# Layer 0's adjacency masks: ScalarE converts two of a tile's four chunks instead of one, VectorE the other two

## The chip, the cores and the metric

The kernel runs on one core of one Trainium2 chip. The metric is the device time of one launch in microseconds (us); several runs of each kernel are taken, and one more execution is profiled. The core's engines are TensorE (PE; its weight loads are PEld), VectorE (DVE), ScalarE (ACT), GpSimd (POOL, idle here) and SyncE (SP), which issues every DMA. Each engine runs its own instructions strictly in the order of the program and waits on semaphores.

## The reference, cut to what matters

Two graph-attention layers over 8192 nodes with 128 features, with a residual after each. The adjacency `adj` is an 8192 x 8192 int32 matrix with about 8 ones in a row, 0.1% of its entries. Layer 0, the one changed here:

```python
h = maximum(layernorm(x), 0)
e = (h @ Ws) @ (h @ Wt).T
alpha = softmax(where(adj > 0, e, -9e15), axis=-1)
x = x + alpha @ (h @ Wc)
```

Layer 1 has the same form with scores `leaky_relu(s1[:, None] + s2[None, :])` and an elu at the end.

## The kernel before, in words

**Tiles and blocks.** A tile is 128 query rows; there are 64. For each tile the matrix `adjB` (a copy of `adj` in which a tile's block of 128 x 8192 lies transposed, key on the partitions) is read in 4 chunks of 16 blocks of 128 keys, 1 MB each. A tile has so few neighbours that layer 0 does not score all 8192 keys: for each block of 128 keys it picks those that are a neighbour of any row of the tile, at most 32, and gathers their keys, values and mask columns with one-hot matrices on TensorE. 64 blocks x 32 slots are 16 groups of 128 slots, on which scores, exponentials and the weighted sum are made.

**A tile's way through the engines** (functions by their names; all in the loop `tile_sweep`, line 332, whose step i handles tile i at its first stages and older tiles at the later ones):

- SP, `load_chunk` (413): loads chunk c of tile i + 1 into `adj_st[:, c]`. Each chunk has a single buffer, so SP first waits until the chunk of the tile before has been converted. `tile_io` (442) issues the four loads in order, then the stores of the one-hot matrix (`store_pick`), of the gathered mask (`store_mask`), of the finished rows, and the next load of rows.
- Conversion of a chunk from int32 to a one-byte mask `mask_8`: by VectorE in line 1327 (chunks 0, 1, 2; values +0.5 and -0.5) and by ScalarE in line 1019 (chunk 3; `Sign` gives +1 and -1). Two sets of constants undo the different scales: `bare` (1207, 1208) and `off_i[q // 3]` (713).
- VectorE, `indicate` (1330): waits for all four chunks, takes a maximum over the rows of each key (line 1334) and compares it with `bare` (1336). TensorE, `prefix` (700, matmul at 704): running count. VectorE, `place` (1338, line 1343): slot numbers `posx`. In the next step VectorE's `make_pick` (1345, line 1352) makes the one-hot matrix `pick`.
- TensorE gathers keys (`pick_keys`, 668), values (`pick_values`, 680) and mask (`pick_mask`, 695) in four, four and two parts, each into one PSUM bank that ScalarE copies out (`take_keys`, 990; `take_values`, 996; `take_mask`, 1003) before the next part may start. `pick_mask` 0 of step i also waits until `place` of tile i - 1 is done.
- TensorE, `scores` (706, lines 712, 713 and 718) for four groups of slots. VectorE takes two maxima (`part_maximum`, 1361), spreads them (`spread_maximum`, 1367), TensorE transposes (`turn_maximum`, 727), VectorE reduces (`maximum`, 1374, 1377). ScalarE makes the exponentials in two halves (`exps`, 1010); `scores` 2 and 3 of the next tile wait for the second half. TensorE, `weigh` (729, lines 736 and 739): 32 float32 matmuls of the sum. VectorE, `denominator` (1384) and `finish` (1391, 1394).

**The order around the change** is written out by hand in each engine's `tile_step`. With a = i - 2, c = i - 3, d = i - 4:

- PE (743): prefix(i-1), scores(c, 3), pick_values(c, 2), pick_mask(a, 0), pick_keys(a, 1), pick_values(c, 3), pick_mask(a, 1), turn_maximum(c), pick_keys(a, 2), pick_values(a, 0), weigh(d, 0 to 3), pick_keys(a, 3), scores(a, 0), pick_values(a, 1), scores(a, 1), pick_keys(i-1, 0), scores(a, 2).
- ACT (1022): take_values(c, 2), take_mask(a, 0), take_keys(a, 1), take_values(c, 3), take_mask(a, 1), take_keys(a, 2), convert(i), exps(c, 0), take_values(a, 0), take_keys(a, 3), exps(c, 1), take_values(a, 1), take_keys(i-1, 0).
- DVE (1397): spread_maximum(c), convert(i, 0), maximum(c), convert(i, 1), make_pick(i-1), convert(i, 2), denominator(d), indicate(i), finish(d), part_maximum(a, 0), place(i), part_maximum(a, 1).

The first six and the last six steps are unrolled; the rest is a hardware loop of two steps. Layer 1 runs after it, on the masks and one-hot matrices that layer 0 stored; the change does not touch it.

Of the kernel before, what the change touches and what calls it, by code (L numbers as in the profile page):

```python
# [13 lines left out]
ACT = mybir.ActivationFunctionType  # L14
# [28 lines left out]
NO_EDGES = struct.unpack("<f", bytes([0xB0] * 4))[0]  # L43
NO_EDGES_ACT = struct.unpack("<f", bytes([0xB8] * 4))[0]


def gnn_kernel(nc, x, adj, adjB, Ws, Wt, Wc, W1, a1, out, x_mid, sel, sel_pick):
    N = x.shape[0]
    TILES = N // P
# [5 lines left out]
    NB = TILES  # L55
    SB = NB // QB
    QCH = NB // 4
    assert CW == 2 * GW and TILES == 64 and D == P

    with ExitStack() as ctx:  # L60
# [11 lines left out]
        def part(start, words, dt=F32):  # L72
            view = arena[:, start:start + words]
            return view if dt == F32 else view.bitcast(dt)
# [4 lines left out]
        adj_st = part(ADJ, 8192, I32).rearrange("p (c b n) -> p c b n", c=4, n=P)  # L79
# [6 lines left out]
        mask_8 = part(MASK, 4096, F8).rearrange("p (r b n) -> p r b n", r=2, n=P)  # L86
# [8 lines left out]
        m_sel8 = part(MS, 1024, F8).rearrange("p (r s n) -> p r s n", r=2, n=P)  # L95
# [8 lines left out]
        off_i = [part(at, P // 2, BF16) for at in (TOP + 2752, END + 200)]  # L104
        bare = part(END + 264, NB)
# [141 lines left out]
        adj_in = [sem(f"adj_in{c}") for c in range(4)]  # L247
        conv_done = sem("conv_done")
        conv_act = sem("conv_act")
# [12 lines left out]
        mg_done = sem("mg_done")  # L262
# [61 lines left out]
        def wait(eng, s, value):  # L324
            if not (isinstance(value, int) and value <= 0):
                eng.wait_ge(s, value)
# [15 lines left out]
        def there(i, d):  # L342

            return within(i, d, TILES + d)
# [51 lines left out]
        def _(sp):  # L396
# [15 lines left out]

            def load_chunk(t, c):

                if c < 3:
                    wait(sp, conv_done, t * 3 + (c - 2))
                else:
                    wait(sp, conv_act, t)
                rows = adjB[bass.ds(t, 1), :, c * QCH:(c + 1) * QCH, :].rearrange("o p b n -> p (o b) n")
                sp.dma_start(adj_st[:, c, :, :], rows).then_inc(adj_in[c], 16)  # L420

# [20 lines left out]
            def tile_io(i, b):  # L442
                if within(i, 0, TILES - 1):
                    for c in range(4):
                        load_chunk(i + 1, c)
                if there(i, 1):
                    store_pick(i - 1, 1 - b)
                if there(i, 2):
                    store_mask(i - 2, b)
                if there(i, 4):  # L450
                    store_y(i - 4, b)
                if within(i, 4, TILES + 2):
                    load_x(i - 2, b)
                if isinstance(i, int) and i == TILES:
                    sp.wait_ge(conv_done, TILES * 3)
                    sp.wait_ge(conv_act, TILES)
                    sp.wait_ge(y_out[0], 16 * (3 * TILES // 8))
                    sp.wait_ge(y_out[1], 16 * (3 * TILES // 8))
                    load_rows(x_mid, 1, range(3))
# [129 lines left out]
        def _(pe):  # L589
# [116 lines left out]
            def scores(t, b, q):  # L706

                pe.wait_ge(k_evac, t * 4 + (q + 1))
                pe.wait_ge(m_evac, t * 2 + (q // 2 + 1))
                wait(pe, p_done, t * 2 + (q // 2 - 1))  # L710
                dst = s_ps[q]
                nc.tensor.matmul(dst, ones_b[:, :], negc, start=True, stop=False, skip_group_check=True)  # L712
                nc.tensor.matmul(dst, off_i[q // 3], m_sel8[:, b, 4 * q:4 * q + 4, :].rearrange("p s n -> p (s n)"),  # L713
                                 start=False, stop=False, skip_group_check=True)
                for k in range(4):
                    at = (4 * q + k) * P
                    for n, rows in enumerate((cq_hi, cq_lo)):
                        last = nc.tensor.matmul(dst[:, k * P:(k + 1) * P], k_sel[:, at:at + P],  # L718
                                                rows[:, bass.ts(t, P)], start=False, stop=(n == 1),
                                                skip_group_check=True)  # L720
                last.then_inc(sc_done, 1)
# [187 lines left out]
        def _(act):  # L909
# [77 lines left out]
            def take_keys(t, g):  # L987

                act.wait_ge(kg_done, t * 4 + (g + 1))
                nc.scalar.activation(k_sel[:, g * GW:(g + 1) * GW], kg_ps, ACT.Copy).then_inc(k_evac, 1)  # L990
# [20 lines left out]
                                     ps[:, 2 * h:2 * h + 2, :].rearrange("p b n -> p (b n)"), ACT.Exp,  # L1011
                                     bias=neg_max[:, 0:1], scale=1.0 / SCORE).then_inc(p_done, 1)

            def convert(t, b):

                act.wait_ge(adj_in[3], t * 16 + 16)
                wait(act, mg_done, t * 2 - 2)
                act.sem_inc(conv_settled, 1)
                nc.scalar.activation(mask_8[:, b, 3 * QCH:4 * QCH, :], adj_st[:, 3, :, :], ACT.Sign, bias=-0.5, saturate=False  # L1019
                                     ).then_inc(conv_act, 1)  # L1020

            def tile_step(i, b):
                a, c, cb = i - 2, i - 3, 1 - b
                if there(i, 3):
                    take_values(c, cb, 2)
                if there(i, 2):
                    take_mask(a, b, 0)
                    take_keys(a, 1)
                if there(i, 3):
                    take_values(c, cb, 3)  # L1030
                if there(i, 2):
                    take_mask(a, b, 1)
                    take_keys(a, 2)
                if there(i, 0):
                    convert(i, b)
                if there(i, 3):
                    exps(c, 0)
                if there(i, 2):
                    take_values(a, b, 0)
                    take_keys(a, 3)  # L1040
                if there(i, 3):
                    exps(c, 1)
                if there(i, 2):
                    take_values(a, b, 1)
                if there(i, 1):
                    take_keys(i - 1, 0)
# [138 lines left out]
        def _(dve):  # L1185
# [13 lines left out]
            def constants():  # L1199

                dve.wait_ge(const_pool, 4)
                dve.wait_ge(ident_ready, 1)
                nc.vector.tensor_copy(tri[:, :], tri_f[:, :])
                nc.vector.tensor_copy(slots[:, :], slot_i[:, :])
                for n in range(2):
                    nc.vector.tensor_scalar(off_i[n], ident[:, :], OFF * (4, 2)[n], None, ALU.mult)
                nc.vector.memset(bare[:, 0:3 * QCH], NO_EDGES)
                nc.vector.memset(bare[:, 3 * QCH:NB], NO_EDGES_ACT)
                nc.vector.memset(pos_top, 0.0)
                nc.vector.memset(negc, -2.0 * OFF / P).then_inc(const_dve, 1)  # L1210

# [110 lines left out]
            def convert(t, b, c):  # L1322

                dve.wait_ge(adj_in[c], t * 16 + 16)
                wait(dve, mg_done, t * 2 + (c // 2 - 3))
                settle()
                nc.vector.tensor_scalar(mask_8[:, b, c * QCH:(c + 1) * QCH, :], adj_st[:, c, :, :], 0.0, 0.5,  # L1327
                                        ALU.is_gt, ALU.subtract, saturate=False).then_inc(conv_done, 1)

            def indicate(t, b):  # L1330

                dve.wait_ge(conv_done, t * 3 + 3)
                dve.wait_ge(conv_act, t + 1)
                nc.vector.reduce_max(ind_raw[:, :], mask_w[:, b, :, :], AX_X).then_inc(ind_max, 1)  # L1334
                dve.wait_ge(ind_max, t + 1)
                nc.vector.tensor_tensor(ind[:, :], ind_raw[:, :], bare, ALU.is_gt).then_inc(ind_ready, 1)
# [60 lines left out]
            def tile_step(i, b):  # L1397
                e, a, c, d = i - 1, i - 2, i - 3, i - 4
                if there(i, 3):
                    spread_maximum(c)  # L1400
                if there(i, 0):
                    convert(i, b, 0)
                if there(i, 3):
                    maximum(c)
                if there(i, 0):
                    convert(i, b, 1)
                if there(i, 1):
                    make_pick(e, 1 - b)
                if there(i, 0):
                    convert(i, b, 2)  # L1410
                if there(i, 4):
                    denominator(d)
                if there(i, 0):
                    indicate(i, b)
                if there(i, 4):
                    finish(d, b)
                if there(i, 2):
                    part_maximum(a, 0)
                if there(i, 0):
                    place(i)  # L1420
                if there(i, 2):
                    part_maximum(a, 1)
# [351 lines left out]
```

## Time and profile before

| | |
|---|---|
| runs | 1467.81, 1470.81, 1476.16 us; median 1470.81 |
| profiled execution | 1470.75 us; its span from first to last instruction 1469.0 us |
| busy in the span | PE 1283.0 us (87%), DVE 1265.2 (86%), ACT 1039.5 (71%), POOL 1.5 |
| mean granted TensorE clock | 0.966 of full speed |
| layer 0's sweep | about 90 to 975 us of the span |
| layer 1 | about 1060 to 1469 us |
| DMA | 363.20 MB over the span |

A busy share is an average over stages with different limits, and an engine that is busy may still not be what the others wait for. The period of a repeating instruction and the waits by releaser say more. In the rows below a line of a timeline reads: start, length, engine, line of the kernel, operation, output and input, shape, count, and in brackets the idle time before it with what ended it. Ends of matmuls are modelled; differences between starts are firm. An instruction can start up to some 0.1 us before the end of the one before it on the same engine. "issue" is a wait for which the profile shows no releaser.

### The profile page before, as it was taken

The numbers are of one execution on the slowest core, as the hardware profiler recorded it, in microseconds if no ns is written. First come the engines' busy times: TensorE is split into PE (matmuls) and PEld (weight loads), VectorE is DVE, ScalarE is ACT, GpSimd is POOL, SyncE is SP. The second block draws the span as 40 slices with busy tenths as digits, with TensorE's granted clock in tenths as the row PEclk, the third lists the DMA queues.
The fourth block names the chain that finished last, engine by engine and source line by source line (L and its number), as shares of the span: only waits on it lengthen the run. The fifth ranks groups of instructions, "written<-read, shape, count | busy, mean of one in ns | idle before, by whom it ended". The sixth has DMA issues, their size and how long they took to land.

```text
span 1469.0 us, 75909 instructions
## 1 busy us (share of the span) xinstructions
PE 1283.0 (87%) x31819; PEld 1132.6 (77%) x31947; DVE 1265.2 (86%) x2313; ACT 1039.5 (71%) x2064; POOL 1.5 (0%) x11
## 2 busy tenths in 40 slices
PE   2827899999999999999999998967699999999996
PEld 1625778878888888888888887755499999999896
DVE  5877689999999999999999998634699999999996
ACT  2835567667677667676767676539599989998885
POOL 0000000000000000000000000000000000000000
PEclk9967899999999999999999999988899999999998
DMA  7049889999999999999999999440132444244432
GB/s 238 1 195 333 281 309 359 372 370 368 380 373 381 372 370 387 362 382 369 375 373 372 374 382 363 145 115 1 45 108 85 120 115 114 87 118 118 117 89 70
DMA packets 114312, 363.20 MB, mean 247 GB/s; under 512 B 11504, under 2 KB 44528, under 8 KB 81392
## 3 DMA queue, kind: packets, MB, share of 16 engines
q1 hardware_dynamic: 114160, 361.02, 68.9%
q8 instruction: 115, 1.88, 0.6%
q14 instruction: 37, 0.30, 0.1%
HBM read 319.03 MB, written 41.94 MB: 246 GB/s over the span
## 4 chain that ended last, share of the span: by engine, by line
PE 46%; DMA 19%; DVE 15%; issue 11%; ACT 7%; SPq 1%; DVEq 1%; ACTq 0%
DMA arena<-in_adjB 17%; PE ps L819 16%; PE ps L806 9%; PE ps L718 4%; DVE arena L1352 4%; DVE arena L1327 4%; PE ps L739 3%; PE ps L713 3%; PE ps L680 3%; DVE mx L1361 2%; ACT arena L1010 2%; ACT arena L915 2%; PE ps L668 2%; PE ps L712 1%; SPq L420 1%
## 5 line engine op out<-in xcount | busy, mean ns | idle before, releaser
L739 PE MATMUL ps<-arena 128*128 128x129 f32 x2048 | 253.1, 283 | 6.0 <-issue 6.0
L739 PEld LDWEIGHTS ps<-arena 128*128 128x128 f32 x2048 | 244.5, 198 | 6.2 <-issue 6.2
L819 PE MATMUL ps<-arena 128*128 128x129 f32 x2048 | 243.0, 277 | 1.1 <-issue 1.1
L996 ACT ACTIVATE arena<-ps 128x512 f32<-128x512 f32 x256 | 153.1, 598 | 125.3 <-PE ps L680 125.2
L1327 DVE TENSOR_SCALAR arena<-arena 128x2048 fp8e4<-128x2048 int32 x192 | 234.8, 1224 | 6.6 <-PE ps L695 3.1
L819 PEld LDWEIGHTS ps<-arena 128*128 128x128 f32 x2048 | 234.6, 192 | 1.4 <-issue 1.4
L1500 DVE TENSOR_SCALAR arena<-arena 128x128 f32<-128x128 f32 x768 | 202.5, 340 | 23.0 <-issue 14.0
L1019 ACT ACTIVATE arena<-arena 128x2048 fp8e4<-128x2048 int32 x64 | 122.3, 1911 | 97.8 <-DMA arena<-in_adjB 97.8
L990 ACT ACTIVATE arena<-ps 128x512 f16<-128x512 f32 x256 | 153.9, 601 | 50.4 <-PE ps L668 50.2
L718 PEld LDWEIGHTS ps<-arena 128*128 128x128 f16 x2048 | 137.5, 99 | 62.8 <-issue 3.6
L1361 DVE TENSOR_REDUCE mx<-ps 128x1 f32<-128x1024 f32 x128 | 155.8, 1217 | 34.0 <-PE ps L718 33.3
L680 PE MATMUL ps<-arena 128*32 128x128 f16 x8192 | 164.8, 222 | 13.4 <-issue 5.7
L1060 ACT ACTIVATE arena<-ps 128x396 f32<-128x396 f32 (+1 forms) x384 | 148.2, 463 | 25.8 <-PE ps L806 25.6
L806 PE MATMUL ps<-arena 128*32 128x132 f16 x8192 | 152.0, 224 | 14.8 <-ACT arena L1060 6.3
L1010 ACT ACTIVATE arena<-ps,neg_max 128x1024 f32<-128x1024 f32 x128 | 142.0, 1110 | 25.2 <-PE ps L739 25.1
L718 PE MATMUL ps<-arena 128*128 (+1 forms) x2048 | 157.9, 220 | 0.0
L806 PEld LDWEIGHTS ps<-arena 128*32 128x32 fp8e4 x8192 | 129.4, 97 | 33.9 <-issue 17.9
L1334 DVE TENSOR_REDUCE arena<-arena 128x64 f32<-128x2048 f32 x64 | 146.3, 2286 | 6.0 <-ACT arena L1019 3.5
L1509 DVE SCALAR_TENSOR_TENSOR arena<-arena 128x1024 f32<-128x1024 fp8e4 x128 | 151.0, 1217 | 0.5 <-ACT arena L1077 0.3
L668 PE MATMUL ps<-arena 128*128 128x32 fp8e4 x4096 | 143.3, 177 | 7.0 <-DVE arena L1352 6.6
L680 PEld LDWEIGHTS ps<-arena 128*32 128x32 fp8e4 x8192 | 121.1, 97 | 34.5 <-issue 17.9
L1352 DVE TENSOR_TENSOR arena<-arena 128x2048 fp8e4<-128x2048 f16 x64 | 146.2, 2284 | 0.1
(166 smaller groups left out, 1399.1 us busy)
## 6 DMA issues: line engine op xcount, KB each, us to landing
arena<-in_adjB SPq DMA_DIRECT2D x256, 1024.0 KB, 7.4
sel_pick<-arena SPq DMA_DIRECT2D x64, 256.0 KB, 9.4
sel<-arena SPq DMA_DIRECT2D x64, 256.0 KB, 9.5
arena<-sel_pick SPq DMA_DIRECT2D x64, 256.0 KB, 3.7
arena<-sel SPq DMA_DIRECT2D x64, 256.0 KB, 2.8
x_t<-in_x SPq DMA_DIRECT2D x64, 64.0 KB, 8.1
x_mid<-y_t SPq DMA_DIRECT2D x64, 64.0 KB, 8.4
arena<-x_mid SPq DMA_DIRECT2D x8, 512.0 KB, 5.0
```

Of the source, the lines that this page charges most:

```text
L668: last = nc.tensor.matmul(kg_ps[:, k * SLOT:(k + 1) * SLOT], kp[:, g * SB + k, :], pick[:, b, g * SB + k, :], start=True, stop=True)
L680: last = nc.tensor.matmul(vg_ps[j * SLOT:(j + 1) * SLOT, s * D:(s + 1) * D], pick[:, b, k, :], c_vals[:, k, l * D:(l + 1) * D], start=(l = ...
L718: last = nc.tensor.matmul(dst[:, k * P:(k + 1) * P], k_sel[:, at:at + P], rows[:, bass.ts(t, P)], start=False, stop=(n == 1), skip_group_c ...
L739: last = nc.tensor.matmul(pv_ps, p_T[:, s * P:(s + 1) * P], v_sel[:, b, s, :], start=False, stop=(s == SB - 1), skip_group_check=True)
L806: last = nc.tensor.matmul(xg_ps[g % 3][j * SLOT:(j + 1) * SLOT, at:at + XW], pick[:, b, s * QB + j, :], wv[:, s * QB + j, l, :], start=(l ...
L819: last = nc.tensor.matmul(xv_ps[b], w_msk[:, b, s, :], x1_sel[:, b, s, 0:VW], start=False, stop=(s == SB - 1), skip_group_check=True)
L990: nc.scalar.activation(k_sel[:, g * GW:(g + 1) * GW], kg_ps, ACT.Copy).then_inc(k_evac, 1)
L1010: nc.scalar.activation(p_T[:, h * 1024:(h + 1) * 1024], ps[:, 2 * h:2 * h + 2, :].rearrange("p b n -> p (b n)"), ACT.Exp, bias=neg_max[:, ...
L1327: nc.vector.tensor_scalar(mask_8[:, b, c * QCH:(c + 1) * QCH, :], adj_st[:, c, :, :], 0.0, 0.5, ALU.is_gt, ALU.subtract, saturate=False).t ...
L1352: nc.vector.tensor_tensor(pick[:, b, :, :], posx.unsqueeze(2).to_broadcast(wide), slots[:, :].unsqueeze(1).to_broadcast(wide), ALU.is_equa ...
L1361: nc.vector.reduce_max(mx[:, h:h + 1], ps[:, 2 * h:2 * h + 2, :].rearrange("p b n -> p (b n)"), AX_X).then_inc(part_max, 1)
L1500: last = nc.vector.tensor_scalar(w_raw[b][:, k, :], own, x1_sel[:, b, k, D + 2:D + 3], x1_sel[:, b, k, D + 1:D + 2], ALU.mult, ALU.max)
```

## The change: another split and another order of the conversions

ScalarE converts chunks 2 and 3. Chunk 2 stands where chunk 3 stood (before `exps(c, 0)`), chunk 3 after `take_keys(a, 3)` and before `exps(c, 1)`. VectorE loses `convert(i, 2)`, between `make_pick` and `denominator`. The counts on `conv_done` and `conv_act` become two a tile each, and the constants follow the new split.

```diff
 def load_chunk(t, c):
-    if c < 3:
-        wait(sp, conv_done, t * 3 + (c - 2))
-    else:
-        wait(sp, conv_act, t)
+    wait(sp, conv_act if c >= 2 else conv_done, t * 2 + (c % 2 - 1))
...
-nc.tensor.matmul(dst, off_i[q // 3], m_sel8[:, b, 4 * q:4 * q + 4, :]...
+nc.tensor.matmul(dst, off_i[q // 2], m_sel8[:, b, 4 * q:4 * q + 4, :]...
...
-def convert(t, b):
-    act.wait_ge(adj_in[3], t * 16 + 16)
+def convert(t, b, c):
+    act.wait_ge(adj_in[c], t * 16 + 16)
     wait(act, mg_done, t * 2 - 2)
...
 # ACT tile_step
     if there(i, 0):
-        convert(i, b)
+        convert(i, b, 2)
     if there(i, 3):
         exps(c, 0)
     if there(i, 2):
         take_values(a, b, 0)
         take_keys(a, 3)
+    if there(i, 0):
+        convert(i, b, 3)
     if there(i, 3):
         exps(c, 1)
...
-nc.vector.memset(bare[:, 0:3 * QCH], NO_EDGES)
-nc.vector.memset(bare[:, 3 * QCH:NB], NO_EDGES_ACT)
+nc.vector.memset(bare[:, 0:2 * QCH], NO_EDGES)
+nc.vector.memset(bare[:, 2 * QCH:NB], NO_EDGES_ACT)
...
 def indicate(t, b):
-    dve.wait_ge(conv_done, t * 3 + 3)
-    dve.wait_ge(conv_act, t + 1)
+    dve.wait_ge(conv_done, t * 2 + 2)
+    dve.wait_ge(conv_act, t * 2 + 2)
...
 # DVE tile_step
     if there(i, 1):
         make_pick(e, 1 - b)
-    if there(i, 0):
-        convert(i, b, 2)
     if there(i, 4):
         denominator(d)
     if there(i, 0):
         indicate(i, b)
```

## Rows read from the trace of the kernel before

**Rows 1.** Stage: length, PE, PEld, DVE, ACT, POOL busy us, clock, DMA share, GB/s

```profile
98.00:250.00 152.00, 118.13 (x3021) 101.65 (x3043) 117.98 (x147) 86.52 (x121) 0.00 (x0) 0.84 0.91 326
250.00:900.00 650.00, 609.31 (x16491) 537.60 (x16580) 611.74 (x803) 453.74 (x652) 0.00 (x0) 1.00 1.00 374
```

**Rows 2.** Line 1334: count, ns min/median/max, first and last start, in 98:250 and 250:900

```profile
L1334 DVE TENSOR_REDUCE arena<-arena x10: 2285/2286/2287, 106.8 to 242.1; 128x64 f32<-128x2048 f32 x10
...
L1334 DVE TENSOR_REDUCE arena<-arena x50: 2285/2286/2289, 254.9 to 890.8; 128x64 f32<-128x2048 f32 x50
```

**Rows 3.** Who waited for whom in 250:900: us in total, times, longest

```profile
ACT arena L1019 <- DMA arena<-in_adjB: 71.3, 50, 2.6
PE ps L713 <- ACT arena L1010: 32.1, 37, 1.8
...
DVE arena L1334 <- ACT arena L1019: 0.5, 2, 0.3
```

**Rows 4.** The chain that ended last, around 515 us: start, us, what

```profile
515.21 9.73 DMA arena<-in_adjB
```

**Rows 5.** DMA traffic in 250:900

```profile
DMA packets 57817, 242.99 MB, mean 374 GB/s; under 512 B 6424, under 2 KB 19244, under 8 KB 32198
```

**Rows 6.** VectorE in order of time: start, us, line, shape

```profile
513.31 1.22 DVE L1327 TENSOR_SCALAR arena<-arena 128x2048 fp8e4<-128x2048 int32 x1
...
514.65 2.29 DVE L1334 TENSOR_REDUCE arena<-arena 128x64 f32<-128x2048 f32 x1
...
518.94 0.21 DVE L1343 TENSOR_TENSOR arena<-ps,arena 128x64 f16<-128x64 f32 x1
...
520.69 0.29 DVE L1367 SCALAR_TENSOR_TENSOR arena<-mx 128x128 f32<-128x128 f32 x1
```

**Rows 7.** ScalarE in the same stretch; in brackets idle before, and releaser

```profile
514.92 0.60 ACT L990 ACTIVATE arena<-ps 128x512 f16<-128x512 f32 x1
515.40 1.12 ACT L1010 ACTIVATE arena<-ps,neg_max 128x1024 f32<-128x1024 f32 x1
...
517.63 0.60 ACT L990 ACTIVATE arena<-ps 128x512 f16<-128x512 f32 x1 [0.62 <-PE ps L668]
...
525.13 1.91 ACT L1019 ACTIVATE arena<-arena 128x2048 fp8e4<-128x2048 int32 x1 [1.97 <-DMA arena<-in_adjB]
526.95 1.10 ACT L1010 ACTIVATE arena<-ps,neg_max 128x1024 f32<-128x1024 f32 x1
```

**Rows 8.** TensorE in the same stretch

```profile
513.83 0.56 PE L668 MATMUL ps<-arena 128*128 128x32 fp8e4 x16
...
517.04 0.56 PE L668 MATMUL ps<-arena 128*128 128x32 fp8e4 x16
517.66 0.38 PE L713 MATMUL ps<-arena 128*128 128x512 fp8e4 x1
...
519.78 0.43 PE L695 MATMUL ps<-arena 128*32 128x64 f16 x32
...
521.66 0.33 PE L727 MATMUL ps<-ident,arena 128*128 128x128 f32 x1
...
526.58 0.56 PE L668 MATMUL ps<-arena 128*128 128x32 fp8e4 x16
528.32 0.38 PE L713 MATMUL ps<-arena 128*128 128x512 fp8e4 x1 [1.19 <-ACT arena L1010]
```

**Rows 9.** A tile in which VectorE waited for ScalarE's conversion

```profile
603.46 1.91 ACT L1019 ACTIVATE arena<-arena 128x2048 fp8e4<-128x2048 int32 x1 [2.57 <-DMA arena<-in_adjB]
...
605.40 2.29 DVE L1334 TENSOR_REDUCE arena<-arena 128x64 f32<-128x2048 f32 x1 [0.31 <-ACT arena L1019]
```

**Rows 10.** A tile in which TensorE waited for line 1343

```profile
109.68 0.23 DVE L1343 TENSOR_TENSOR arena<-ps,arena 128x64 f16<-128x64 f32 x1 [0.33 <-PE ps L704]
...
110.05 0.62 PE L695 MATMUL ps<-arena 128*32 128x64 f16 x32 [0.41 <-DVE arena L1343]
```

**Rows 11.** A standstill of TensorE in the early stretch

```profile
177.91 0.30 PE L695 MATMUL ps<-arena 128*32 128x64 f16 x8 [3.99 <-issue]
```

More of the change, by code:

```diff
@@ L454, in tile_io @@
                 if isinstance(i, int) and i == TILES:
-                    sp.wait_ge(conv_done, TILES * 3)
-                    sp.wait_ge(conv_act, TILES)
+                    sp.wait_ge(conv_done, TILES * 2)
+                    sp.wait_ge(conv_act, TILES * 2)
                     sp.wait_ge(y_out[0], 16 * (3 * TILES // 8))
@@ L712, in scores @@
                 nc.tensor.matmul(dst, ones_b[:, :], negc, start=True, stop=False, skip_group_check=True)
-                nc.tensor.matmul(dst, off_i[q // 3], m_sel8[:, b, 4 * q:4 * q + 4, :].rearrange("p s n -> p (s n)"),
+                nc.tensor.matmul(dst, off_i[q // 2], m_sel8[:, b, 4 * q:4 * q + 4, :].rearrange("p s n -> p (s n)"),
                                  start=False, stop=False, skip_group_check=True)
@@ L1012, in exps @@
                                      bias=neg_max[:, 0:1], scale=1.0 / SCORE).then_inc(p_done, 1)
-            def convert(t, b):
-                act.wait_ge(adj_in[3], t * 16 + 16)
+            def convert(t, b, c):
+                act.wait_ge(adj_in[c], t * 16 + 16)
                 wait(act, mg_done, t * 2 - 2)
                 act.sem_inc(conv_settled, 1)
-                nc.scalar.activation(mask_8[:, b, 3 * QCH:4 * QCH, :], adj_st[:, 3, :, :], ACT.Sign, bias=-0.5, saturate=False
-                                     ).then_inc(conv_act, 1)
+                nc.scalar.activation(mask_8[:, b, c * QCH:(c + 1) * QCH, :], adj_st[:, c, :, :], ACT.Sign, bias=-0.5,
+                                     saturate=False).then_inc(conv_act, 1)
             def tile_step(i, b):
@@ L1324, in convert @@
                 dve.wait_ge(adj_in[c], t * 16 + 16)
-                wait(dve, mg_done, t * 2 + (c // 2 - 3))
+                wait(dve, mg_done, t * 2 - 3)
                 settle()
```

## The prediction, made before the changed kernel ran

> **What bounds the kernel now.** I read the stages first. Layer 0's sweep runs in its settled part at full granted clock, with VectorE (DVE) busy 94% of the time, TensorE (PE) 94%, ScalarE (ACT) 70% and the DMA engines 100% [rows 1]; before that, from 98 to 250 us, the mean granted clock is 0.84. The reduction of line 1334 runs once a tile, so its first and last start give the tile period [rows 2]: (890.8 - 254.9) / 49 = **12.98 us** in the settled part, and (254.9 - 106.8) / 10 = 14.81 us over the first full tiles. Next the waits of the settled part, 50 tiles [rows 3]: ACT waits 71.3 us for adjacency chunks (1.43 us a tile) and then makes PE wait 32.1 us (0.64 us a tile) for the exponentials behind that conversion. VectorE waits for ScalarE's conversion only twice, 0.5 us in all: line 1334 is reached after the conversion is done. The chain that ended last goes through a chunk load of 9.73 us [rows 4]. So today's cycle is: load of chunk 3, ACT's conversion, exponentials, PE's scores, VectorE's maxima and conversions, next load. The transfers fill all of it: 242.99 MB in 650 us is 374 GB/s [rows 5], or 4.85 MB a tile.
>
> **The change, part by part.**
>
> *Removed from VectorE*: one conversion a tile, 1.22 us long (513.31) [rows 6]. VectorE's work falls from 0.94 x 12.98 = 12.2 to about 11.0 us a tile. That is worth nothing in itself if VectorE then has to wait.
>
> *Added to ScalarE*: one conversion of 1.91 us, the same shape as the one in the trace; the next instruction starts 1.82 us after its start [rows 7]. ScalarE's work goes from 9.1 to 10.9 us a tile, under 12.98, so its load is not the question. The order is.
>
> *Moved*: chunk 2 takes the old place (ahead of the first exponentials). Chunk 3 now stands behind `take_keys(a, 3)`, and that copy waits for PE's `pick_keys(a, 3)`, which PE issues after the whole of `weigh`. But VectorE's `indicate` needs all four chunks. VectorE is in order: behind `indicate` are `finish`, both score maxima, `place`, the spread of the maximum. PE waits for `indicate` (prefix), for `place` (`pick_mask`) and for the spread (`turn_maximum`). A new ring closes within one tile: PE's key group 3, ACT's copy, ACT's conversion, VectorE's `indicate` to `place`, PE's `pick_mask` to the next key group 3.
>
> The ring's length, t = 0 when PE ends key group 3:
> - ACT starts the copy 0.03 later (517.63 against 517.04 + 0.56) [rows 7, 8]: 0.03.
> - The copy holds ACT 0.48 (514.92 to 515.40) [rows 7]: 0.51.
> - Conversion 1.91 [rows 7], and 0.03 until VectorE starts (605.40 against 603.46 + 1.91) [rows 9]: **2.45**.
> - `indicate` start to `place` start, VectorE without a wait: 518.94 - 514.65 = 4.29 [rows 6]: 6.74.
> - `place` 0.21, then 0.14 until a waiting PE starts (110.05 against 109.68 + 0.23) [rows 6, 10]: 7.09.
> - `pick_mask` 0 to key group 3, start to start: 526.58 - 519.78 = 6.80 [rows 8]. The same 6.80 repeats from tile to tile in the settled part. A few tenths of it are PE waiting for ACT's copies of values and keys; as `pick_values` 2 now lies well ahead of the held-up `pick_mask`, I take 6.75, with 6.5 and 6.9 as bounds: 13.84.
> - Key group 3 itself 0.56 [rows 8]: **14.40 us**.
>
> Is VectorE really early? In the tile of the rows `indicate` starts at 514.65, 1.34 after the start of the conversion at 513.31; without the conversion it would be ready near 513.5, while PE ends key group 3 at 513.83 + 0.56 = 514.39 [rows 6, 8]: it stands 0.9 before t = 0 and is let go at 2.45. It waits over 3 us a tile. Does the spread come later than PE needs it? From `place` to the end of the spread are 520.69 + 0.29 - 518.94 = 2.04, so it ends at 8.78 at the latest; PE reaches `turn_maximum` at 7.09 + 521.66 - 519.78 = 8.97 [rows 6, 8]. No, though by little: I allow 0.2 for it in the upper bound. So the bounds of the period are 14.1 and 14.7; 14.40 is the plain sum.
>
> *What of the ring hides in today's period*: nothing. Today `indicate` depends only on a conversion in front of PE's `weigh`; the new ring has `weigh` and the conversion in series.
>
> *The loads*: chunks are single buffered, so a load follows its conversion, and SP issues it behind waits in program order. Chunk 3 is converted by 2.42, so its load is issued at about 2.6, and it is wanted at 14.40 + 0.51 = 14.9. Chunk 2's conversion starts some 1.1 after `turn_maximum` (key group 2 and its copy), near 10.1, and is over at 12.0, which is -2.4 of the next tile: its load has 12.5 us. Even at today's 9.73 us [rows 4] both land in time. SP holds the stores of pick, mask and rows and the next row load behind chunk 3's wait; they need some 3 us of issue, and the next chunk 0 is freed only at about 10, behind the spread (8.5) and its own conversion. Hidden; if the transfers were slower by over 2 us, chunk 2 would show as an ACT wait. ACT's wait for chunks and PE's 0.64 us for the first exponentials go: these start at 12.0 and PE wants them at 14.4. This gain vanishes in the ring.
>
> *One-off edits*: two memsets of another split, the scaled identity chosen by q // 2, SP's waits (one a chunk as before): the same instructions, 0. At the start of the sweep VectorE has one conversion less before its first `indicate`: 1.1 us gained.
>
> *The sum*: 49 settled periods x (14.40 - 12.98) = 69.6. In the first ten, PE also stands still for up to 3.99 us inside a group without a releaser ("issue") [rows 11]; the old mean exceeds 12.98 by 1.8. Such a stall adds fully if it falls in the ring's PE part, about half the tile, and is swallowed by the new waits elsewhere: 14.4 + 1.2 = 15.6 against 14.81, + 8 (bounds 0 and + 20). Three last periods: + 4. Start: - 1. Together + 81. The profiled execution took 1470.75 (span 1469.0 + 1.75), the median of the runs is 1470.81, so no shift: **1551 us**.
>
> **The rivals.**
>
> *A clock that falls.* PE will stand idle 2 us a tile in three pieces (second exponentials, `indicate`, `place`), all within 4 us of light work. In the early stretch, where PE stalled about once a tile, the granted clock's mean was 0.84 and the tile 1.83 us longer [rows 1, 2]. Against it: in the settled part PE waits up to 1.8 us in one piece [rows 3] and the clock stays at 1.00 (2.4 GHz). If it fell each tile: 49 x 1.83 more = **1641 us**. 0.10. The Trainium skill's page "TensorE: Matmul & The Clock Gate", section "A second HAM failure mode: psum-queue depth-cycling", says that frequent small gaps between groups of matmuls can make the clock swing; the settled rows do not show that here.
>
> *A weaker ring.* If VectorE's hold-up were absorbed, the second exponentials remain: 0.51 + 1.82 + (528.32 - 526.95 = 1.37) = 3.70 until `scores` 2, then 526.58 + 0.56 - 517.66 = 9.48 to the next t = 0 [rows 7, 8]: 13.18 a tile, 49 x 0.20 + 4 = **1485 us**. Nothing in the order of the code frees `place` from `indicate`, so 0.05.
>
> *Bound by transfers, no change.* The DMA engines are 100% busy at 374 GB/s [rows 1, 5]. If 12.98 us is the transfers' own time and the new ring were shorter than I add up, nothing would move: **1471 us**. It needs the ring under 12.98, 1.4 less than my sum. 0.06. The Trainium skill ("DMA: Bandwidth & Descriptors", "Where 436 GB/s comes from") puts the HBM side's limit near 358 GB/s; 4.85 MB would then take 13.5 us, a floor that would forbid any gain. The trace's 374 lies above that figure.
>
> *Faster.* ACT converts chunk 2 without waiting for chunk 3, and PE no longer waits for the first exponentials: 12.98 - 0.64 = 12.34 a tile, 49 x 0.64 = **1439 us**. It decides at `indicate`: it holds if chunk 3's conversion ends before VectorE is ready, over 3 us earlier than I place it, that is if PE's key group 3 did not stand before it. For it: 71.3 us of ACT's waits. Against it: the program order. 0.07.
>
> **How the numbers follow.** Forecast 0.72, clock 0.10, weak ring 0.05, no change 0.06, faster 0.07. Bounds of the forecast: 49 x 1.1 + 0 + 3 - 1 = + 56 and 49 x 1.7 + 20 + 5 - 1 = + 107, so 1527 to 1578. For 8 in 10 the range leans toward the clock: 1522 to 1592. A measurement tells about 0.5% from no change. Slower 0.87, same 0.06, faster 0.07.
>
> **What would show it.** Right: line 1334 waits for ACT's conversion 2 to 4 us in each tile; its period is 14.1 to 14.7; PE waits at the prefix (line 704) for line 1336 and at `pick_mask` (line 695) for line 1343; DMA share near 0.9; ACT no longer waits for chunks; clock 1.00 after 250 us. Wrong: a period near 13.2 with no wait at line 704 (weak ring), ACT waiting for chunk 2 (transfers), a clock under 0.95 in the settled part, or line 1334 starting without a wait.

## The result, and the profile after

The changed kernel takes 1556.86 us (median of 4 runs, 1556.58 to 1564.46) against 1470.84 us in the same comparison: a ratio of 1.0587, 95% interval 1.0558 to 1.0617, so 86 us slower. The forecast was 1551 us and slower. The profiled execution took 1557.05 us with a span of 1555.1.

The first lines of its page, busy us by engine, and further down the groups of the two conversions and of `indicate` (line 1333 now; before it was 1334):

```profile
PE 1306.6 (84%) x31819; PEld 1137.7 (73%) x31947; DVE 1190.8 (77%) x2249; ACT 1156.2 (74%) x2128; POOL 1.5 (0%) x11
...
L1333 DVE TENSOR_REDUCE arena<-arena 128x64 f32<-128x2048 f32 x64 | 146.3, 2286 | 162.3 <-ACT arena L1016 162.3
L1016 ACT ACTIVATE arena<-arena 128x2048 fp8e4<-128x2048 int32 x128 | 244.6, 1912 | 14.3 <-DMA arena<-in_adjB 14.3
...
L1326 DVE TENSOR_SCALAR arena<-arena 128x2048 fp8e4<-128x2048 int32 x128 | 156.9, 1227 | 5.3 <-DMA arena<-in_adjB 2.7
```

ScalarE has 128 conversions, VectorE 128; each takes what one took before. VectorE's busy time is down by 74 us and ScalarE's up by 117 us, and neither is what the time went to. What is new is the wait in front of line 1333: 162.3 us, all of it put down to ScalarE's conversion. Before it was 3.5 us over the whole span.

Where the 86 us lie follows from the same line's starts. First its 50 instances from 250 us on, then all 64:

```profile
L1333 DVE TENSOR_REDUCE arena<-arena x50: 2285/2286/2287, 251.5 to 959.4; 128x64 f32<-128x2048 f32 x50
```

```profile
L1333 DVE TENSOR_REDUCE arena<-arena x64: 2285/2286/2289, 92.9 to 1022.2; 128x64 f32<-128x2048 f32 x64
```

Tile 10 starts at 251.5 where before it was 242.1 [rows 2]: 9.4 us late. Tile 59 starts at 959.4, so a settled tile takes (959.4 - 251.5) / 49 = **14.45 us** against 12.98 [rows 2]. The last tile starts at 1022.2. Layer 1 and what lies between are as long as before: line 1506, its first VectorE work, starts at 1145.6, and the span ends 409.5 later; before it was 408.6.

The waits of the settled part, in total, times and longest (50 tiles), which answer to [rows 3]:

```profile
ACT arena L993 <- PE ps L677: 144.5, 50, 4.1
DVE arena L1333 <- ACT arena L1016: 126.6, 50, 2.5
PE ps L710 <- ACT arena L1007: 48.5, 50, 1.0
...
PE ps L701 <- DVE arena L1335: 30.2, 50, 0.6
...
DVE invs L1383 <- PE ps L736: 26.7, 49, 1.0
```

ACT's wait for a chunk, 71.3 us before [rows 3], is gone from the list. VectorE now waits 126.6 / 50 = 2.53 us a tile for the conversion, and TensorE waits at the scores behind the second exponentials (0.97 a tile) and at the prefix behind line 1335 (0.60, beside an "issue" share).

One turn of the ring, first ScalarE, then VectorE, then TensorE (start, length, and in brackets the wait and its releaser); these answer to [rows 6 to 8]:

```profile
611.93 0.60 ACT L987 ACTIVATE arena<-ps 128x512 f16<-128x512 f32 x1 [0.58 <-PE ps L665]
612.42 1.90 ACT L1016 ACTIVATE arena<-arena 128x2048 fp8e4<-128x2048 int32 x1
614.22 1.11 ACT L1007 ACTIVATE arena<-ps,neg_max 128x1024 f32<-128x1024 f32 x1
```

```profile
600.03 2.29 DVE L1333 TENSOR_REDUCE arena<-arena 128x64 f32<-128x2048 f32 x1 [2.53 <-ACT arena L1016]
...
614.43 2.29 DVE L1333 TENSOR_REDUCE arena<-arena 128x64 f32<-128x2048 f32 x1 [2.53 <-ACT arena L1016]
...
618.72 0.22 DVE L1342 TENSOR_TENSOR arena<-ps,arena 128x64 f16<-128x64 f32 x1
...
628.78 2.29 DVE L1333 TENSOR_REDUCE arena<-arena 128x64 f32<-128x2048 f32 x1 [2.53 <-ACT arena L1016]
```

```profile
611.33 0.56 PE L665 MATMUL ps<-arena 128*128 128x32 fp8e4 x16
...
615.69 0.38 PE L710 MATMUL ps<-arena 128*128 128x512 fp8e4 x1 [0.97 <-ACT arena L1007]
...
617.12 0.20 PE L701 MATMUL ps<-arena 128*128 128x64 f16 x1 [0.61 <-DVE arena L1335]
...
619.04 0.42 PE L692 MATMUL ps<-arena 128*32 128x64 f16 x32
...
625.69 0.56 PE L665 MATMUL ps<-arena 128*128 128x32 fp8e4 x16
```

Key group 3 starts on TensorE at 611.33, ScalarE copies it from 611.93, converts chunk 3 from 612.42, VectorE is let go at 614.43, `place` starts at 618.72, TensorE's `pick_mask` at 619.04, and the next key group 3 at 625.69: 14.36 us for one turn. The chain of waits of this kernel, as the profile follows it back, takes the same way through ScalarE and VectorE; these are pieces of that turn:

```profile
612.42 1.91 ACT arena L1016
...
614.43 2.30 DVE arena L1333
...
616.75 0.23 DVE arena L1335
...
617.12 0.20 PE ps L701
...
622.22 3.63 PE ps L736 x32
```

From line 701 on it stays on TensorE and leaves out `place`, because the pause in front of `pick_mask` is too short for this view. The starts show that `place` holds it all the same: in 44 of the tiles 12 to 57, 46 in all, `pick_mask` starts 0.10 us after the end of `place` (the other two are tiles in which the clock fell), and the prefix 0.14 us after the end of line 1335 in all 46. So the turn closes by two ways at nearly the same time, and the later one is `place`.

### The profile page after: what moved, and what is told of

It reads as the page before. It is cut to its first block, busy times and chain, and to the rows that moved or that the text cites. A ratio compares the mean times of both kernels' runs of the same rounds, so it can differ in the third digit from the quotient of the medians.

```text
span 1555.1 us, 75853 instructions
## 1 busy us (share of the span) xinstructions
PE 1306.6 (84%) x31819; PEld 1137.7 (73%) x31947; DVE 1190.8 (77%) x2249; ACT 1156.2 (74%) x2128; POOL 1.5 (0%) x11
## 4 chain that ended last, share of the span: by engine, by line
PE 65%; DVE 13%; ACT 12%; issue 7%; DMA 2%; SPq 1%; DVEq 0%; ACTq 0%
PE ps L736 15%; PE ps L816 15%; DVE arena L1333 9%; PE ps L803 9%; ACT arena L1016 8%; PE ps L677 7%; PE ps L665 5%; PE ps L692 3%; PE ps L715 2%; ACT arena L912 2%; PE ps L709 2%; PE ps L710 1%; PE ps L724 1%; DVE arena L1335 1%; PE ps L701 1%
## 5 line engine op out<-in xcount | busy, mean ns | idle before, releaser
L1333 DVE TENSOR_REDUCE arena<-arena 128x64 f32<-128x2048 f32 x64 | 146.3, 2286 | 162.3 <-ACT arena L1016 162.3
L1016 ACT ACTIVATE arena<-arena 128x2048 fp8e4<-128x2048 int32 x128 | 244.6, 1912 | 14.3 <-DMA arena<-in_adjB 14.3
L1497 DVE TENSOR_SCALAR arena<-arena 128x128 f32<-128x128 f32 x768 | 202.8, 344 | 23.6 <-issue 13.9
L803 PE MATMUL ps<-arena 128*32 128x132 f16 x8192 | 152.3, 224 | 15.6 <-ACT arena L1059 6.9
L1326 DVE TENSOR_SCALAR arena<-arena 128x2048 fp8e4<-128x2048 int32 x128 | 156.9, 1227 | 5.3 <-DMA arena<-in_adjB 2.7
L803 PEld LDWEIGHTS ps<-arena 128*32 128x32 fp8e4 x8192 | 129.6, 97 | 34.7 <-issue 18.5
L710 PE MATMUL ps<-arena 128*128 128x512 fp8e4 x256 | 98.5, 385 | 66.7 <-ACT arena L1007 62.1
```

The source lines that it names most:

```text
L803: last = nc.tensor.matmul(xg_ps[g % 3][j * SLOT:(j + 1) * SLOT, at:at + XW], pick[:, b, s * QB + j, :], wv[:, s * QB + j, l, :], start=(l ...
L1016: nc.scalar.activation(mask_8[:, b, c * QCH:(c + 1) * QCH, :], adj_st[:, c, :, :], ACT.Sign, bias=-0.5, saturate=False).then_inc(conv_act, 1)
L1497: last = nc.vector.tensor_scalar(w_raw[b][:, k, :], own, x1_sel[:, b, k, D + 2:D + 3], x1_sel[:, b, k, D + 1:D + 2], ALU.mult, ALU.max)
```

## The experiments

Ten kernels were run, each compared with before on its own chip. The tile period is taken from the first and last start of the `indicate` reduction between 250 and 850 us (before: 250 and 900; changed: 250 and 970). Seven runs took a time outside the range that was expected: e3 by 2.5 us, e6, e7 and e9 5 to 13 us shorter with a period near the expected one, and e5, e8 and e10 because their period was missed.

| run | edit | time, us | ratio to before (95%) | tile period, us |
|---|---|---|---|---|
| before | | 1470.8 | 1 | 12.98 |
| changed | | 1556.9 | 1.059 (1.056 to 1.062) | 14.45 |
| e1 | 3:1 split, ScalarE's one conversion late | 1551.3 | 1.056 (1.052 to 1.059) | 14.30 |
| e2 | 2:2, both early | 1481.1 | 1.007 (1.005 to 1.010) | 13.20 |
| e3 | 2:2, second one ahead of the key copy | 1482.5 | 1.009 (1.006 to 1.012) | 13.20 |
| e4 | changed + spare VectorE work | 1557.7 | 1.060 (1.056 to 1.063) | 14.50 |
| e5 | e3 + `finish` ahead of `indicate` | 1483.8 | 1.009 (1.006 to 1.012) | 13.13 |
| e6 | before, loads halved | 1421.6 | 0.967 (0.964 to 0.971) | 12.41 |
| e7 | changed, loads halved | 1542.7 | 1.050 (1.046 to 1.053) | 14.53 |
| e8 | e5, loads halved | 1457.9 | 0.992 (0.990 to 0.994) | 13.13 |
| e9 | before, chunk 3 loaded ahead of chunk 2 | 1434.6 | **0.974 (0.972 to 0.976)** | **12.42** |
| e10 | changed + `finish` ahead of `indicate` | 1553.4 | 1.056 (1.053 to 1.059) | 14.37 |

### e1: the place without the split

```diff
 # ACT tile_step, kernel of before
-    if there(i, 0):
-        convert(i, b)
     if there(i, 3):
         exps(c, 0)
     if there(i, 2):
         take_values(a, b, 0)
         take_keys(a, 3)
+    if there(i, 0):
+        convert(i, b)
```

> The split of before (VectorE converts chunks 0, 1 and 2, ScalarE chunk 3), but chunk 3's conversion stands where the change puts its second one, behind the copy of key group 3. Ring theory: the place alone makes the ring, and VectorE's third conversion fits into its wait, so the tile period is 14.37 us as in the changed kernel and the time 1550 to 1560 us. Rival, the cost is ScalarE's 1.9 us of added work or the 2:2 split: the period stays near 13.0 and the time near 1471 us. Rival, the cost is partly the work: halfway, about 1510 us.

1551.3 us, 14.30 us a tile. One conversion on ScalarE, three on VectorE, no work added anywhere, and nearly the whole loss is there. So the place makes the loss, 1.32 of the 1.47 us a tile, without ScalarE's added 1.9 us and without the 2:2 split. The waits of the settled part show the same hand-over, shorter because VectorE's third conversion stands in front of it (81.1 / 42 = 1.93 us a tile instead of 2.53):

```profile
DVE arena L1334 <- ACT arena L1019: 81.1, 42, 1.9
```

### e2 and e3: the split without the place

```diff
 # e2, ACT tile_step, changed kernel
     if there(i, 0):
         convert(i, b, 2)
+        convert(i, b, 3)
     ...
-    if there(i, 0):
-        convert(i, b, 3)
```

> The changed kernel with both of ScalarE's conversions in the old place, back to back ahead of the first exponentials. Ring theory: no ring through the weighing; indicate starts about 4.8 us after the third key group starts on TensorE and the ring is about 11.4 us, so it does not bind. The first exponentials start 1.82 us later than they could, TensorE waits about 0.7 us for them on top of its own 12.38 us: period 13.1 us, 1465 to 1485 us. Rival, ScalarE's added work costs wherever it stands: 14.4 us a tile, about 1555 us. Rival, relief of VectorE is worth something: period 12.4, 1440 us.

```diff
 # e3, ACT tile_step, changed kernel
     if there(i, 2):
         take_values(a, b, 0)
-        take_keys(a, 3)
     if there(i, 0):
         convert(i, b, 3)
+    if there(i, 2):
+        take_keys(a, 3)
```

> The changed kernel with the second conversion moved up by one instruction, ahead of the copy of key group 3 and behind the first values. Ring theory: the conversion no longer waits for the weighing; from the start of key group 2 on TensorE: exponentials at 3.1, values 4.1, conversion 4.6 to 6.5, indicate to place 4.3, TensorE from pick_mask to key group 2 2.2: period about 13.0 us, 1460 to 1480 us. If the transfers set 12.98 us by themselves it cannot be under that. Rival, two conversions on ScalarE cost by their work: about 1555 us.

1481.1 and 1482.5 us. Moving the conversion by a single instruction (e3) takes 1.25 us a tile back. Both come out at the same 13.20, a little over the 13.1 and 13.0 expected, and each by its own wait. In e2 TensorE waits at `scores` 0 for the first exponentials, 32.7 / 49 = 0.67 us a tile (0.7 was expected), and VectorE doesn't wait for ScalarE at all:

```profile
PE ps L709 <- ACT arena L1007: 32.7, 49, 0.7
```

In e3 VectorE still waits, 66.4 / 49 = 1.36 us a tile:

```profile
DVE arena L1334 <- ACT arena L1016: 66.4, 49, 1.4
```

`pick_mask` starts 0.10 us after the end of `place` in all of the tiles 12 to 57, as in the changed kernel: e3 is held by a ring of the same kind, entered one copy earlier.

### e4: spare work for VectorE

```diff
 # DVE tile_step, changed kernel, behind make_pick
+    if there(i, 0):
+        dve.wait_ge(proj_hi, PREP)
+        nc.vector.reduce_max(spare[:, 0:1], c_vals[:, 0:4, :].rearrange("p b v -> p (b v)"), AX_X
+                             ).then_inc(spare_done, 1)
+        dve.wait_ge(spare_done, i + 1)
```

> The changed kernel with a spare reduction of 128x1024 on VectorE (about 1.2 us, its result unused) between make_pick and the denominator, where before had the third conversion. Ring theory: VectorE waits 2.5 + 0.5 us a tile there, the spare work is swallowed: period 14.37 and time within 0.3% of the changed kernel's 1557 us. Rival, VectorE's load matters in the changed kernel: + 1.1 us a tile, about 1625 us.

1557.7 us against 1556.9: a reduction of about the removed conversion's size costs nothing. It is taken out of the wait, which shrinks from 2.53 to 69.5 / 42 = 1.65 us a tile. What the change took off VectorE was worth nothing in the changed kernel.

```profile
DVE arena L1335 <- ACT arena L1018: 69.5, 42, 2.0
```

### e5 and e10: shortening VectorE's part

```diff
 # DVE tile_step (e5: on e3; e10: on the changed kernel)
+    if there(i, 4):
+        finish(d, b)
     if there(i, 0):
         indicate(i, b)
-    if there(i, 4):
-        finish(d, b)
```

> The order of the run with the conversion ahead of the key copy (period 13.20 us, VectorE waiting 1.4 us a tile ahead of indicate), and VectorE's finish moved from behind indicate to ahead of it, into that wait: 0.70 us leave the ring, which falls to 12.5 us. Transfer theory: 4.85 MB a tile need about 12.98 us by themselves, so the period stops at 12.95 to 13.0 and the time at 1466 to 1473 us. Rival, the transfers of before only followed the cycle through chunk 3: period 12.5 us, 1443 to 1450 us, faster than both kernels.

> The changed kernel with finish moved ahead of indicate, the place of the second conversion untouched. Ring theory with two closings: the closing by place gets 0.70 shorter, but the closing by the prefix (indicate, prefix, scores 3, values 2, pick_mask) holds at about 14.37 - 0.46 = 13.9 us: 1530 to 1536 us. Rival, only the closing by place binds: 13.67 us, 1517 to 1524 us. Rival, finish is not in the ring: 14.37, 1557 us.

Both misses. e5 stays at 13.13 us, where 12.5 or 12.98 was expected; e10 takes 14.37 with the tiles in which the clock fell (three of 15.5 us), and 14.28 without, where 13.9 was expected. In e10 the turn closes by another way. TensorE's rows:

```profile
604.31 0.56 PE L665 MATMUL ps<-arena 128*128 128x32 fp8e4 x16
...
608.66 0.38 PE L710 MATMUL ps<-arena 128*128 128x512 fp8e4 x1 [0.97 <-ACT arena L1007]
...
610.09 0.20 PE L701 MATMUL ps<-arena 128*128 128x64 f16 x1 [0.60 <-DVE arena L1335]
...
611.85 0.43 PE L692 MATMUL ps<-arena 128*32 128x64 f16 x32
```

Line 701, the prefix, is held until 610.09 by `indicate`, and `pick_mask` follows 1.76 later, not held by `place` any more (line 1342 ends at 611.22). The tiles without a fall take 14.28: the closing by the prefix was only 0.1 us behind the closing by `place`. The forecast had it 0.46 behind. In before, where neither end is held, `pick_mask` starts 1.46 us after the prefix in every tile; in e10, behind a held prefix, it is 1.65 and 1.76 in turn.

e5 fails for the same reason. Its rows:

```profile
612.87 0.23 DVE L1336 TENSOR_TENSOR arena<-arena 128x64 f16<-128x64 f32 x1
...
613.24 0.20 PE L701 MATMUL ps<-arena 128*128 128x64 f16 x1
```

The prefix starts 0.14 us after the end of line 1336, and so in all of the tiles 12 to 57, while `pick_mask` now starts 0.52 to 0.69 us after the end of `place` instead of 0.10. Moving `finish` shortens the way from `indicate` to `place` and leaves the way from `indicate` to the prefix as it was. That one was only 0.07 us shorter than the other: 13.20 becomes 13.13. No run shortens the closing by the prefix.

### e6, e7, e8: halved loads

```diff
 # load_chunk
+    n = QCH if isinstance(t, int) and t == 0 else QCH // 2
-    rows = adjB[bass.ds(t, 1), :, c * QCH:(c + 1) * QCH, :].rearrange("o p b n -> p (o b) n")
-    sp.dma_start(adj_st[:, c, :, :], rows).then_inc(adj_in[c], 16)
+    rows = adjB[bass.ds(t, 1), :, c * QCH:c * QCH + n, :].rearrange("o p b n -> p (o b) n")
+    sp.dma_start(adj_st[:, c, 0:n, :], rows).then_inc(adj_in[c], 16)
```

These three leave out half of the adjacency from tile 1 on; in its place stand the entries of tile 0.

> The kernel of before, every chunk load after the first tile's cut to half its blocks; the other half of a chunk keeps the first tile's entries. Transfers fall to some 7 us a tile, arithmetic and order are unchanged. Transfer theory: without them before runs at its own 12.38 us a tile, the length of its shortest tiles: 1435 to 1443 us. Rival, chunk lateness is no part of before's 12.98: unchanged, 1471 us.

> The changed kernel with the same halved loads. Ring theory: no transfer is in its ring, period 14.35 to 14.40 us and the time 1550 to 1557 us. Rival, part of the loss is in late chunks: several us a hundred less per tile, under 1530 us.

> The kernel with finish ahead of indicate, loads halved as before. Ring theory: period 12.4 to 12.5 us whatever the full loads gave, 1436 to 1450 us. Rival, another ring (the exponentials or the spread of the maximum) holds it at 12.9 or more, near 1468 us.

Without half the bytes before runs at 12.41 us a tile, the length of its shortest tiles (12.38 us). Its time is 49 us shorter, 13 more than the low end expected: 27 us come from the tiles 10 to 59, as forecast, 18 from the first ten and 4 from the last. The changed kernel's plain tiles do not move, 14.40 and 14.39 or 14.34 between starts:

```profile
616.34 2.29 DVE L1334 TENSOR_REDUCE arena<-arena 128x64 f32<-128x2048 f32 x1 [2.53 <-ACT arena L1017]
...
630.73 2.29 DVE L1334 TENSOR_REDUCE arena<-arena 128x64 f32<-128x2048 f32 x1 [2.53 <-ACT arena L1017]
```

Its ring holds no transfer. Its mean of 14.53 is above the changed kernel's because TensorE's clock fell in more of its tiles: six times between tiles 10 and 59 instead of three, at 1.1 us each. Its 14 us come from the start of the sweep: tile 10 starts at 238.3 where the changed kernel had it at 251.5. The next 49 tiles take 3 us more, by the clock, and the last ones 3 us less.

```profile
L1334 DVE TENSOR_REDUCE arena<-arena x10: 2285/2286/2287, 102.7 to 238.3; 128x64 f32<-128x2048 f32 x10
```

e8 answers e5: 13.13 us with full and with half loads, so transfers are not what stops e5. The expectation's rival (another ring at 12.9 or more) holds for the period; the time of 1457.9 us lies between the two that were named. Against e6 the pair says one thing more: without late chunks the 2:2 split in e5's order costs 0.7 us a tile (13.13 against 12.41). Against before most of that does not show, since before loses 0.56 us a tile to its late chunk.

### e9: the order of two loads

```diff
 # tile_io, kernel of before
-    for c in range(4):
+    for c in (0, 1, 3, 2):
         load_chunk(i + 1, c)
```

> The kernel of before with one edit: SP loads ScalarE's chunk 3 ahead of VectorE's chunk 2. In before chunk 3 lands as ScalarE asks for it, chunk 2 lands some 4 us early. Lateness theory: before loses its 0.6 us a tile only because the chunk with no slack is loaded last; now it lands near 12 us after the first load's issue, wanted at 13, and the period falls to 12.4 to 12.6 us: 1440 to 1452 us, faster than both kernels. Transfer theory: 4.85 MB take 12.9 us whatever the order, the wait moves to another chunk: 1463 to 1471 us.

1434.6 us, ratio 0.974 (0.972 to 0.976): faster than both kernels, with before's split and ScalarE's old order, and 5 us under the range that was expected: 27 of the 35 us lie in the tiles 10 to 59, 6 in the first ten. First the period's line, then busy time by stage (length, PE, PEld, DVE, ACT, POOL, clock, DMA share, GB/s):

```profile
L1334 DVE TENSOR_REDUCE arena<-arena x49: 2285/2286/2286, 248.3 to 844.3; 128x64 f32<-128x2048 f32 x49
```

```profile
250.00:850.00 600.00, 592.70 (x15933) 516.33 (x16030) 584.26 (x776) 443.92 (x628) 0.00 (x0) 1.00 1.01 390
```

(844.3 - 248.3) / 48 = 12.42 us a tile. The DMA share reads 1.01, as it read 1.00 before, yet the same engines now move 390 GB/s instead of 374 [rows 1]. ScalarE no longer waits for a chunk in the settled part.

Why the order matters, in before's rows: chunk 3's load is issued at 515.21 and lands at 524.94 [rows 4], and ScalarE, which has waited for it, starts on it at 525.13 [rows 7]. VectorE starts on chunk 2 at 526.06, and without a wait:

```profile
526.06 1.22 DVE L1327 TENSOR_SCALAR arena<-arena 128x2048 fp8e4<-128x2048 int32 x1
```

Its load is issued at 514.69 and takes 7.5 us to land, at 522.15: it lay there for 3.9 us. Over the tiles 15 to 57 the medians from landing to the start of the conversion are 0.18 us for chunk 3 and 4.6 us for chunk 2. In e9 they are 0.9 and 1.0 us: the slack is shared out, and neither engine waits for a chunk.

## Why the prediction was right

- *The ring.* Forecast 14.40 us a turn, measured 14.35 and 14.40 in turn; mean 14.45. Its terms, in the order of the working: copy started 0.60 after the start of key group 3 (0.59 forecast), 0.49 to the conversion (0.48), 2.01 until VectorE starts (1.94), 4.29 to `place` (4.29), 0.32 to `pick_mask` (0.35), 6.65 to key group 3 (6.75). e1 shows that the place alone makes it, e3 that one instruction's move undoes most of it, e7 that no transfer is in it.
- *VectorE's relief is worth nothing.* Shown by e4. The forecast of VectorE's wait was right in sum and wrong in place. It had all of it ahead of `indicate`, "over 3 us", and VectorE ready 0.9 us before t = 0. It left out that `denominator`, which stands in between, needs the end of `weigh`: VectorE waits 0.54 us a tile there (line 1383, 26.7 / 49), is through at 611.90, just when TensorE's key group 3 ends, and then waits 2.53. The 14.40 does not depend on it.
- *The sum.* Settled part: 49 x 1.42 = 69.6 forecast, 959.4 - 251.5 - 49 x 12.98 = 71.9 measured. The early tiles and the start: + 8 - 1 forecast, + 9.4 measured at tile 10: tile 0 starts 1.0 earlier (92.9 against 93.9), as forecast, and the ten tiles behind it take 10.4 longer. The last tiles: from tile 59 to the last start 1022.2 - 959.4 = 62.8 us, which makes + 4.6 (+ 4 forecast), since the three together are the 85.9 us by which the last tile starts later (936.3 before).
- *Where it fell short.* The forecast was 5 us low. Half of that is in the first ten tiles (10.4 where 8 was put). The other half is the clock, which was set at 1.00 for the whole settled part. It fell to half three times for about 3.4 us, near 269, 385 and 501, each time in the tile's stretch behind the new waits, and the tiles there took 15.5 to 15.6 us: 3.5 us more in all. The other tiles, at 14.35 and 14.40, were 1.2 us shorter in sum than forecast. The falling clock was a rival; it came true at a small part of its price. The stretch of the first fall, and the one behind it:

```profile
269.00:272.50 3.50, 3.50 (x90) 2.79 (x90) 3.16 (x6) 0.74 (x2) 0.00 (x0) 0.52 0.86 313
272.50:277.00 4.50, 4.50 (x139) 4.26 (x136) 4.25 (x5) 4.46 (x7) 0.00 (x0) 1.00 0.80 268
```

The Trainium skill's page "TensorE: Matmul & The Clock Gate", section "A second HAM failure mode: psum-queue depth-cycling", says that small gaps between groups can make the clock swing; this row agrees for 3 tiles of 50, and e4, e7 and e10 have such tiles too, while e1 at 14.30 us has none. The halved clock costs 1.1 to 1.2 us a tile where it strikes.
- *The signs.* DMA share 0.94 where near 0.9 was named, no wait for chunks (chunks 2 and 3 land 3.6 and 4.7 us before their conversions start, medians of the tiles 15 to 57), waits at lines 1333, 701 and 710 as named. The one at `pick_mask` shows in the list only as 0.16 of "issue" in every other tile; the 0.10 us from the end of `place` to its start is what shows it.
- *The rivals.* The weaker ring's 13.18 us were worked out for the second exponentials. That e2 and e3 come to 13.20 is chance: e2 is held at `scores` 0 by the first exponentials, e3 by VectorE's wait for the conversion. "Bound by transfers" is refuted as a statement about before too, by e9.
- *A claim of the working that did not hold*: that the transfers fill all of today's cycle. They were busy all of it and still had room; what cost 0.56 us a tile (12.98 against e9's 12.42) was that the chunk without slack was loaded last. The Trainium skill ("DMA: Bandwidth & Descriptors", "Where 436 GB/s comes from") gives about 358 GB/s, a core's half of what its HBM stack delivers, as the side that binds. For this kernel on one core that is no limit: 390 GB/s over 600 us were measured in e9. The forecast did not rest on it.

## What to carry to other kernels

When work moves to another engine, look first at what stands in front of its new place in that engine's order, and follow the wait once round: 1.9 us of work on an engine that was idle 30% of the sweep cost 1.4 us a tile because it was put behind a copy that waits for the longest stretch of another engine. Add the turn up from start to start of rows, and add up the next closings as well, since in e5 and e10 the shortened turn fell onto one that was 0.1 us behind. A DMA share of 100% is no proof of a bound: compare when each transfer lands with when it is wanted, and load first what has no slack.

## What was not expected of the hardware

- The DMA engines' share reads 1.00 at 374 GB/s and 1.01 at 390 GB/s; only the landing times against the demand told the two apart.
- Halved loads took 13 us off the first ten tiles of the changed kernel. In that stretch TensorE stands still inside groups without a releaser [rows 11]; the longest such pause at line 677 is 4.6 us, in e7 (line 678) 1.6 us. The profile's queue for instructions moves 15 packets between 98 and 250 us in either kernel and none between 250 and 850. So these pauses may be the loading of instructions, slowed by the stream of adjacency data; no run isolates it.
- TensorE's clock fell in three of some 50 equal tiles, where waits of 0.97 and 0.60 us stand within 1.5 us of each other; the three lie 116 us apart, which is eight tiles. In e4 and e7 it fell in every eighth tile of the settled part. At 14.30 us a tile (e1), with the same two waits at 0.75 and 0.53 us, it never fell there. Why only some tiles are hit was not tried.
